# Gate units issued inside the ticks of the convolution and head units of a hybrid state-space, mixture-of-experts and sparse-projection layer

## The reference

```
zxbcdt = hidden_states @ in_proj_w.T
gate = zxbcdt[..., :DIN]
xBC = zxbcdt[..., DIN:DIN + CONV_DIM]
conv = conv_general_dilated(xBC, conv_w, ...)             # causal, 4 taps, one channel each
xBC = silu(conv + conv_b)
x, B, C = split(xBC)                                       # x: 128 heads of 64; B, C: 128 states a group
Y_diag = einsum('bhcij,bcjhd->bcihd', (C B^T) * L, x * dt) # inside a chunk
Y_off = einsum(C, states, exp(A_cumsum))                   # from the chunks before
y = Y_diag + Y_off + D * x
y = y * silu(gate)
y = y * rsqrt(mean(y * y over the group) + EPS) * norm_w
out = y @ out_proj_w.T
```

## Time and profile before

| what | us |
|---|---|
| median of 3 runs | 2342.14 (2337.01 to 2342.54) |
| the profiled execution, time | 2340.48 |
| its span, first to last instruction | 2338.4 |
| PE busy | 2096.4 (90%) |
| DVE busy | 1585.1 (68%) |
| ACT busy | 1231.7 (53%) |
| POOL busy | 1152.2 (49%) |

### The profile page before, as it was taken

How to read it: one execution, slowest core, us unless ns; L and a number is a source line. 1 busy time by engine, 2 the same in 40 slices (tenths; PEclk the granted TensorE clock), 3 DMA queues, 4 the chain that set the end, 5 groups by cost and what they waited for, 6 DMA issues and landing times.

```text
span 2338.4 us, 39600 instructions
## 1 busy us (share of the span) xinstructions
PE 2096.4 (90%) x11776; PEld 1731.7 (74%) x11776; DVE 1585.1 (68%) x2766; ACT 1231.7 (53%) x2680; POOL 1152.2 (49%) x987
## 2 busy tenths in 40 slices
PE   3889998989999989999998899899989888989897
PEld 2678777877777777777787778777777767767775
DVE  5797489739973996498659956984698463167314
ACT  2676367627762775377437744864476323522341
POOL 0377247814781578157716661765277414330332
PEclk7999999999999999999999999999999999999999
DMA  2343034203421342044113412331243027941894
GB/s 69 123 127 90 19 100 131 73 29 104 128 63 37 111 130 64 24 118 134 48 49 109 128 37 70 104 113 37 71 115 101 19 100 279 404 140 44 283 392 150
DMA packets 143765, 261.22 MB, mean 112 GB/s; under 512 B 19521, under 2 KB 35905, under 8 KB 143553
## 3 DMA queue, kind: packets, MB, share of 16 engines
q1 hardware_dynamic: 134848, 231.35, 31.2%
q0 software_dynamic: 7520, 24.65, 3.3%
q10 hardware_dynamic: 1184, 2.62, 0.3%
HBM read 233.38 MB, written 25.17 MB: 111 GB/s over the span
## 4 chain that ended last, share of the span: by engine, by line
PE 40%; issue 25%; POOL 21%; DVE 11%; ACT 1%; another core or an unknown queue 1%; POOLq 0%; DMA 0%; DVEq 0%; SPq 0%; ACTq 0%
PE bank L1475 25%; PE bank L1758 5%; POOL gt L681 5%; POOL Y L692 5%; POOL cv L699 4%; POOL Y L675 3%; PE bank L1608 3%; POOL wl L659 2%; PE bank L1770 2%; PE bank L1622 1%; DVE mem L1226 1%; POOL mem L650 1%; DVE Y L1184 1%; PE bank L1745 1%; DVE mem L1152 1%
## 5 line engine op out<-in xcount | busy, mean ns | idle before, releaser
L1475 PE MATMUL bank<-xh,wh 128*128 128x512 f32 x1288 | 522.2, 405 | 17.2 <-POOL wl L659 10.3
L1475 PE MATMUL bank<-xh,wl 128*128 128x512 f32 x1288 | 504.1, 391 | 0.0
L1475 PE MATMUL bank<-xl,wh 128*128 128x512 f32 x1288 | 503.5, 391 | 0.0
L659 POOL TENSOR_TENSOR wl<-raw,wh 128x512 fp32r<-128x512 f32 x144 | 183.9, 1282 | 511.1 <-ACT wh L857 510.5
L1184 DVE SCALAR_TENSOR_TENSOR Y<-bank,cpar,Y 128x511 f32<-128x511 f32 (+2 forms) x384 | 287.0, 747 | 21.3 <-ACT Y L874 11.1
L1475 PE MATMUL bank<-wh,ah 128*128 128x512 f32 x576 | 241.7, 420 | 65.7 <-DVE wl L1139 24.3
L1475 PEld LDWEIGHTS bank<-xh,wh 128*128 128x128 f32 x1288 | 243.2, 189 | 65.8 <-issue 12.2
L1475 PEld LDWEIGHTS bank<-xh,wl 128*128 128x128 f32 x1288 | 242.6, 188 | 52.6
L1475 PEld LDWEIGHTS bank<-xl,wh 128*128 128x128 f32 x1288 | 243.5, 189 | 45.1 <-issue 0.5
L1249 DVE TENSOR_TENSOR al<-Y,ah 128x512 fp32r<-128x512 f32 x128 | 108.8, 856 | 201.0 <-ACT ah L937 201.0
L650 POOL TENSOR_TENSOR mem<-mem,hpt 128x384 f32<-128x384 f32 x128 | 106.7, 834 | 275.9 <-DVE mem L1152 259.3
(11 more groups left out here) (211 smaller groups left out, 4228.7 us busy)
## 6 DMA issues: line engine op xcount, KB each, us to landing
mem<-c_rows SPq DMA_DIRECT2D x176, 256.0 KB, 3.6
mem<-wffn_d SPq DMA_DIRECT2D x62, 512.0 KB
E<-c_rows SPq DMA_DIRECT2D x256, 96.0 KB, 2.8
raw<-wconv_d SPq DMA_DIRECT2D x80, 256.0 KB, 2.8
cv<-c_rows SPq DMA_DIRECT2D x80, 256.0 KB, 3.6
raw<-wgate_d SPq DMA_DIRECT2D x64, 256.0 KB, 2.7
raw<-wout_d SPq DMA_DIRECT2D x64, 256.0 KB, 2.6
slots_y<-quad SPq DMA_DIRECT2D x62, 256.0 KB
```

What stands on the lines that cost most here:

```text
L659: inc(pool.tensor_tensor(wl[:, W_SLOT[p], :], raw[:, R_SLOT[p], :], wh[:, W_SLOT[p], :], ALU.subtract), w_lo)
L1475: got = mm(out, l, r, start=first and n == 0, stop=last and n == 2)
```

## The change

The gate units move. In the kernel after, gate unit n is issued in tick n+12, the out-projection in ticks 28 to 35, and a group has 36 ticks; ticks 12 to 19 have a convolution unit **and** a gate unit. The list `BIG` orders the 44 big units as they now come (conv 12, gate 0, conv 13, gate 1, ...), and the three banks go round in that order. PE issues a tick's gate unit behind the state sums and transposes, and ahead of diag and off. With it come:

- the tanh of the convolution's silu is written into the unit's own PSUM bank, and DVE ends the silu of every unit (`conv_ok`; POOL's two instructions for 11 of them go); the bank is free only after that, where it was free after the taps;
- the products with the masked C B^T move from DVE to POOL, the sum of squares from POOL to DVE;
- diag has one bank and is issued chunk by chunk, its two heads in turn; the transposes have two banks; there are eight `L` buffers;
- the exp of the row that scales off is made once for all groups ahead of the loop and loaded from a second tensor in device memory, `e_rows`;
- the x pieces 4 to 7 go by sequence first, which lets half of the out-projection's rows be ready early, and the weight pieces are loaded and rounded in a new order.

Lines of the kernel after that answer to lines before: 1482 for 1475 (the big matmuls), 1562 for 1565 (state sums), 1590 for 1593 (transposes), 1620 for 1608 (diag), 1634 for 1622 (off); on DVE 1196 for 1184 (taps), 1205 for 1193 (end of silu), 1164 for 1152, 1179 and 1184 for 1167 and 1172 (states), 1242 for POOL's 699.

```diff
-        TR, DG, ST, OF = 3, (4, 5), 6, 7
+        TR, DG, ST, OF = (3, 5), 4, 6, 7
...
-        EARLY = 9
-        conv_early = counted("conv_early", EARLY)
-        conv_vt = counted("conv_vt", NCONV - EARLY)
-        conv_late = counted("conv_late", NCONV - EARLY)
...
-        LR, ER = 6, 3
+        LR, ER = 8, 3
...
+        ULIST = [(t, b) for t in range(XT // 2) for b in range(BATCH)] \
+            + [(t, b) for b in range(BATCH) for t in range(XT // 2, XT)]
+        CLIST = [(t, b) for t in range(2) for b in range(BATCH)] + [(t + 2, b) for t, b in ULIST]
+        GATE_AT, OUT_AT = 12, 28
+        TICKS = OUT_AT + TT
+        BIG = []
+        for k in range(TICKS):
+            BIG += [("conv", k)] if k < NCONV else []
+            BIG += [("gate", k - GATE_AT)] if 0 <= k - GATE_AT < NGATE else []
+            BIG += [("out", k - OUT_AT)] if k >= OUT_AT else []
+        J = {what: j for j, what in enumerate(BIG)}
+
...
+        W_TICK = [0, 0, 1, 3, 5, 7, 7, 8, 9, 9, 10, 10, 11, 12, 13, 14, 15, 17, 20, 21, 22, 23, 24, 25, 26, 28]
...
-            if q < NCONV:
-                wait(eng, taps, i, 3 * q + 3)
-            elif q < NCONV + NGATE:
-                wait(eng, gate_ok, i, q - NCONV + 1)
-            else:
-                wait(eng, res_ok, i, q - NCONV - NGATE + 1)
+            kind, n = BIG[q]
+            wait(eng, dict(conv=conv_ok, gate=gate_ok, out=res_ok)[kind], i, n + 1)
...
+        def tr_bank(what):
+            return TR[TR_ORDER.index(what) % 2]
...
-            last = TR_ORDER[n - 1]
+            last = TR_ORDER[n - 2]
...
+                    u = k - A_ - 1
+                    if 0 <= u < UNITS:
+                        pair, b = unit(u)
+                        for h in range(2):
+                            n = 2 * u + h
+                            now(pool, decay_ok, i, n + 1)
+                            if n == 0:
+                                now(pool, g_ok, i, 2)
+                            inc(pool.tensor_tensor(L[n % LR], L[n % LR],
+                                    G[:, b * CH:(b + 1) * CH, :].rearrange("p c i -> p (c i)"),
+                                    ALU.mult), lg_ok)
...
-                    kc = k - 1
-                    if EARLY <= kc < NCONV:
-                        now(pool, conv_th, i, kc + 1)
-                        dst = piece(*conv_unit(kc))
-                        inc(pool.tensor_tensor(gt[:, kc % 2, :], dst, gt[:, kc % 2, :], ALU.mult), conv_vt)
-                        now(pool, conv_vt, i, kc - EARLY + 1)
-                        inc(pool.tensor_tensor(dst, dst, gt[:, kc % 2, :], ALU.add), conv_late)
-
...
-                    n = k - 3 - NCONV
-                    if BATCH <= n < NGATE:
-                        now(pool, sq_ok, i, n + 1)
-                        if n >= 2 * BATCH:
-                            now(pool, ss_add, i, n - 2 * BATCH + 1)
-                        inc(pool.tensor_tensor(acc[:, n % 2, :], acc[:, n % 2, :], sq[:, n % 2, :], ALU.add), ss_add)
...
+            n = step(nc.scalar.activation(v_hm, c_hm, ACT.Exp))
+            act.wait_ge(act_step, n)
+            act.dma_start(e_rows.rearrange("g h n -> (g h) n"), v_hm).then_inc(scr_rows, 16)
...
-                        e_arrived(act, i, u)
-                        inc(nc.scalar.activation(E[:, u % ER, :], E[:, u % ER, :], ACT.Exp), e_ok)
...
-                        inc(nc.scalar.activation(gt[:, kc % 2, :], src, ACT.Tanh, scale=0.5), conv_th)
+                        inc(nc.scalar.activation(bank[big_bank(J["conv", kc])][:, :], src, ACT.Tanh, scale=0.5), conv_th)
...
-                    if 0 <= kc < EARLY:
+                    if 0 <= kc < NCONV:
                         tile, b = conv_unit(kc)
                         dst = piece(tile, b)
                         now(dve, conv_th, i, kc + 1)
-                        inc(STT(dst, gt[:, kc % 2, :], 1.0, dst, ALU.add, ALU.mult), conv_early)
+                        inc(STT(dst, bank[big_bank(J["conv", kc])][:, :], 1.0, dst, ALU.add, ALU.mult), conv_ok)
 
...
-                        inc(STT(dst, dst, dcol[:, pair:pair + 1], bank[DG[u % 2]][:, :], ALU.mult, ALU.add), ydiag_ok)
+                        inc(STT(dst, dst, dcol[:, pair:pair + 1], bank[DG][:, :], ALU.mult, ALU.add), ydiag_ok)
...
-                        now(dve, e_ok, i, u + 1)
+                        e_arrived(dve, i, u)
...
-                    u = k - A_ - 1
-                    if 0 <= u < UNITS:
-                        pair, b = unit(u)
-                        for h in range(2):
-                            n = 2 * u + h
-                            now(dve, decay_ok, i, n + 1)
-                            if n == 0:
-                                now(dve, g_ok, i, 2)
-                            inc(TTn(L[n % LR], L[n % LR],
-                                    G[:, b * CH:(b + 1) * CH, :].rearrange("p c i -> p (c i)"),
-                                    ALU.mult), lg_ok)
...
-                    if NCONV <= k < NCONV + NGATE:
-                        n = k - NCONV
+                    n = k - GATE_AT
+                    if 0 <= n < NGATE:
                         now(dve, gate_th, i, n + 1)
-                        last = STT(gt[:, n % 2, :], gt[:, n % 2, :], 1.0, bank[big_bank(k)][:, :],
+                        last = STT(gt[:, n % 2, :], gt[:, n % 2, :], 1.0, bank[big_bank(J["gate", n])][:, :],
                                    ALU.add, ALU.mult)
                         inc(last, gate_ok)
+                    n = k - 3 - GATE_AT
+                    if BATCH <= n < NGATE:
+                        b = GATES[n][1]
+                        now(dve, sq_ok, i, n + 1)
+                        if n > BATCH:
+                            now(dve, ss_add, i, n - BATCH)
+                        inc(TTn(acc[:, b, :], acc[:, b, :], sq[:, n % 2, :], ALU.add), ss_add)
+                    for t, m in y_evac(k):
+                        now(dve, y_hi, i, 2 * t + m + 1)
+                        inc(TTn(al[:, m, :, :], rows_of(t, m), ah[:, m, :, :], ALU.subtract), y_lo)
...
-                    elif k < NCONV + NGATE:
-                        tile, b = gate_unit(k)
-                        half, col = tile // 4, tile % 4 * P
-                        if tile % 4 == 0 and b == 0:
-                            piece_split(pe, i, CONV + KT * half + KT - 1)
-                        big_bank_free(pe, i, k)
-                        for kt in range(KT):
-                            s = W_SLOT[CONV + KT * half + kt]
-                            last = three(out, xh[:, kt, b * SEQ:(b + 1) * SEQ], xl[:, kt, b * SEQ:(b + 1) * SEQ],
-                                         wh[:, s, col:col + P], wl[:, s, col:col + P], kt == 0, kt == KT - 1, False)
-                        inc(last, big_mm)
-                    else:
-                        t = k - NCONV - NGATE
...
+                    n = k - GATE_AT
+                    if 0 <= n < NGATE:
+                        tile, b = GATES[n]
+                        j = J["gate", n]
+                        half, col = tile // 4, tile % 4 * P
+                        if n % XT == 0:
+                            piece_split(pe, i, PNO["gate", KT * half + KT - 1])
+                        big_bank_free(pe, i, j)
+                        for kt in range(KT):
+                            s = W_SLOT[PNO["gate", KT * half + kt]]
+                            last = three(bank[big_bank(j)][:, :], xh[:, kt, b * SEQ:(b + 1) * SEQ],
+                                         xl[:, kt, b * SEQ:(b + 1) * SEQ],
+                                         wh[:, s, col:col + P], wl[:, s, col:col + P], kt == 0, kt == KT - 1, False)
+                        inc(last, big_mm)
 
                     u = k - D_
...
-                        if u >= 2:
-                            now(pe, ydiag_ok, i, u - 1)
+                        if u:
+                            now(pe, ydiag_ok, i, u)
                         else:
                             before(pe, ydiag_ok, i, UNITS)
-                        for h in range(2):
-                            for c in range(CH):
+                        for c in range(CH):
+                            for h in range(2):
                                 hs = slice(h * HD, (h + 1) * HD)
-                                last = mm(b4(DG[u % 2])[hs, c, :], xs[:, u % 3, c, hs],
+                                last = mm(b4(DG)[hs, c, :], xs[:, u % 3, c, hs],
                                           L[(2 * u + h) % LR][:, c * P:(c + 1) * P], start=True, stop=True)
```

More of the change, by code:

```diff
@@ L404, in conv_unit, with rows_gated @@
         def conv_unit(k):
-            return k // 2, k % 2
-        def gate_unit(k):
-            return unit(k - NCONV)
+            return CLIST[k]
+        GATES = ULIST
+        def rows_gated(eng, i, t, m):
+            now(eng, y_gated, i, max(n for n, (tile, b) in enumerate(GATES) if tile // 4 == m and b == t // CH) + 1)
         def piece(tile, b):
@@ L637, in _ @@
             with pool.Fori(0, GROUPS) as i:
```

(18 more changed lines are left out.)

174 lines of the change are left out of this document (84 added, 90 removed).

## The result

The kernel after takes 2516.35 us (median of 4 runs, 2505.77 to 2520.63) where the one before takes 2339.57: ratio 1.0751, 95% interval 1.071 to 1.0792. The forecast was 2472. The profiled execution took 2505.8 us, with a span of 2504.0.

What follows compares the result with a forecast made beforehand. PE, busy 90% of the span, was taken to bound the kernel. 207 + 112 + 12 + 10 + 16 - 164 - 62 = +131 us on 2340.5 gave 2472 us; the 8-in-10 range was 2350 to 2600.

Steps and rivals of the forecast that it cites:

- The wait: Ticks 13 to 19: PE's gate unit waits 3.7 us for DVE's end of silu, 7 times a group, +207 us.
- The clock: Ticks 13 to 19: matmuls behind each wait run at a slower clock, 2.0 us a tick, +112 us.
- Small ones: Minor effects across the group's ticks, entering the forecast sum as +12, +10 and +16 us, others taken as 0.
- (a): Ticks 0 to 5: convolution banks come free one tick later, 1.5 us a group, +12 us.
- (c): Ticks 9 to 12: ACT's two weight roundings a tick make conv 13 and gate 0 2 us late, +16 us.
- (b): Merged ticks: a 128x512 matmul behind a small one takes 0.31 instead of 0.23 us, 15 gates more, +10 us.
- What goes: PE's old waits at transposes and out-projection, 132.0 us, and the slow clock behind them, 32 us, vanish: -164 us.
- Diag in turns: Alternating heads overlaps the array halves in diag, gaining 0.56 us a unit, partly counted in ticks 20 to 26: -62 us.
- Ticks 20 to 27 about as long as before: Claim that these ticks, with products moved from DVE to POOL, keep about their old length.
- the first (the ring does not close): Rival: gates run inside the ticks, PE the only limit, 2153 us, or 2254 with half the wait; chance 0.14.
- the ring: Ticks 13 to 19: gate awaits end of silu, behind states needing this tick's state sums; next convolution queues behind the gate.
- The hold of DVE's sum of squares by POOL: Possible shared-port lockout ahead of DVE's states: a further 1.3 us hold would add 0.5 a tick, 28 us.

Runs made afterwards that it cites:

- e5: Kernel after with the x transposes issued nine times in ticks 13 to 19, useless work filling PE's wait for the end of silu: 2406.2 us.
- e3: Kernel after with ACT's tanh ahead of the convolution start and DVE's end of silu ahead of states and taps, behind tick 12: 2183.4 us.
- e4: Kernel after with gates back at ticks 20 to 35 and out-projection at 36 to 43, the rest of the change kept: 2153.0 us.
- e11: e4 with ACT's rounding of the gated rows moved ahead of the tick's square: 2151.5 us.
- e2: Kernel after with diag issued one head after the other again: 2544.8 us.
- e6: Kernel after with PE's gate unit behind diag and off in its tick instead of ahead of them: 2331.6 us.
- e9: e4 with diag issued one head after the other: 2214.1 us.

## Why the prediction was right

The named mechanism is what the runs show, and nearly all of the loss; its terms can be laid beside the rows:

- **The wait: +207, measured 212.** 3.79 us, 7 a group: 56 of the 80 waits for 1205.
- **The clock: +112, measured about 106 in the rows, 110 to 115 by e5.** In the second group the seven gate units take 5.42, 4.54, 4.54, 4.45, 5.42, 4.54, 4.54 us, 4.78 on the mean instead of the 2.95 of e5, and the seven diags 0.5 us more in all: 13.3 us a group. That it falls so near is partly luck: the old stalls gave 1.7 us (8.4 slow matmuls) on the mean and 2.8 at most, and the 2.0 a tick was chosen between them.
- **Small ones (a) and (c): +12 and +16, measured 24** (13.4 us of waits for `quad` in the first ticks of a group, and the other 24 waits for 1205, 10.4 us). (b), +10, was not measured apart; PE's busy time in e3, with merged ticks, is 10.0 us above that in e4, without them, which agrees with it.
- **What goes: -164, of which some 25 stayed.** The step failed where it says that the low half of the rows would come in time because it is ahead of the norm: 1245 still holds PE for 16.4 us and the last weight piece for 4.0. On ACT the rows stand behind a square that waits for DVE's sum of squares; I had looked at DVE's order alone, and e11 shows that ACT's order is a part of it. The slow clock behind these stalls, 32 us of the term, did not go everywhere either: in the out-projection's stretch of groups 3, 5 and 7 the granted clock is 0.97 over 58.7 us each, some 5 us in all. The rest of the 32 was not measured apart.
- **Diag in turns: -62, in PE's work -58 (e2) to -64** (128 x 0.5), but net of what it lets PE wait for only 28 to 36. The forecast took POOL for the next limit in ticks 20 to 26 and let 0.4 us a unit come through; DVE was the limit, as the next line shows. Diag takes 1.03 us, not under 1.0.
- **"Ticks 20 to 27 about as long as before" failed by a little**: the state sums wait 18.4 us in 32 times for DVE's states of the tick before. DVE is busy 41.49 of 43.20 us in that stretch, where the tick has gate, sum of squares and weight piece together. In the second group these ticks take 44.1 us, 47.4 before; without diag's 2.8 and the old waits' 2.2 they should have taken 42.4.

With what was measured the sum is 212 + 106 + 24 + 10 + 18 - 139 - 64 = +167, on 2340.5 that is 2507.5, against 2505.8 measured; the 10 and 27 us of the 139 are still the forecast's. The forecast's +131 was short by the 25 that stayed and the 18 that came, more than by anything else. The runs of the kernel lie between 2505.8 and 2520.6; the profiled one is the lowest of them, the median 10 us above it. So groups are 249.1 us apart and not 244, and of the 132 us of waits that were to be gone 20 are left. Two slips in the working change nothing: 366.39 is the start of the row behind the taps, which end at 366.47, and diag's term comes to 62.7.

Of the rivals, the first (the ring does not close) is what e3 shows: 2183.4, where I had worked out 2153 for PE as the only limit. The 30 us between them are about the same waits for 1245, the weight piece and the states (16.5, 4.0 and 17.0 us) that the forecast lacks. That e4, another kernel, takes 2153.0 is chance. The hold of DVE's sum of squares by POOL did not reach the ring: DVE stood 1.67 us ahead of the state sums.

The Trainium skill, "TensorE: Matmul & The Clock Gate", section "A second HAM failure mode: psum-queue depth-cycling", says that short idles between groups of matmuls make the clock go to and fro between its two levels: the trace agrees, with 0.85 in ticks 13 to 19 against 1.00 around them. e6 shows that not each such idle does it: behind five of the second group's seven waits of 1.90 to 1.97 us no matmul is slow.

What stays open is the distance of 30 us between e3 and e4, in part. By the reciprocals a group takes (1698.4 - 240.0) / 7 = 208.3 us in e3 and (1669.7 - 236.8) / 7 = 204.7 in e4, so the 3.6 us lie in the repeated part. PE's lists of waits account for half: e3 has 17.0 us of state sums that wait for DVE's states, which e4 has not, and 9.6 of gate units that wait for the end of silu where e4 has 1.4; e4 has 7.3 and 2.7 us in two entries of its own. The net is 15 us. PE's busy time is 10.0 us longer in e3, which fits the prediction's (b), the switches between small and large matmuls, but was not tested apart. The last 4 us no entry names.

## What to carry to other kernels

When two streams of work share a ring of buffers, write down for each use which earlier use it takes the buffer from, and where in the consumer's program of the same tick the releasing row stands. If it stands behind a row that needs this tick's product of the producer, the engines run in turns, however much room the sums of busy time show. Such a ring is broken by moving the releasing row (333 us here) or by a further buffer (224 us here, because the buffer was taken from the transposes and closed another ring there). Moving the row needs no buffer. Relieve an engine first and then look whether the merge is still needed: here it was not.

## What the runs showed of the hardware

**Two halves of the array.** Eight float32 matmuls of 64 columns (sixteen passes in the rows), heads in turn, take 1.03 us (after); head by head 1.52. Switching in and out included, that is 0.13 us a matmul against 0.19. The Trainium skill, "TensorEngine Tiling (Array Packing)", section "Key Properties", says that different tiles can load and multiply in parallel; the rows agree. Which head comes next decides, not the number of matmuls: e9, where PE is the limit, pays 61 us for the other order.

**DVE held by POOL.** In e4 POOL's gating product

```profile
424.39 1.68 POOL L714 TENSOR_TENSOR Y<-Y,gt 128x512 f32<-128x512 f32 x1 [1.89 <-DVE gt L1233]
```

runs beside DVE's rows. DVE's row 1245 with two SBUF inputs, 0.69 us where it runs alone (at 435.86), lasts until 0.54 us after POOL's end (424.39 + 1.68 = 426.07, 424.83 + 1.78 = 426.61):

```profile
424.23 0.68 DVE L1242 TENSOR_TENSOR cv<-cv,quad 128x512 f32<-128x512 f32 x1
424.83 1.78 DVE L1245 TENSOR_TENSOR al<-Y,ah 128x512 fp32r<-128x512 f32 x1
```

The Trainium skill, "SBUF — State Buffer", section "SBUF: two separate sides", says that a VectorE instruction with two SBUF inputs and a GpSimd instruction that reads SBUF shut each other out for a whole instruction; these rows agree. The rows with a PSUM operand (1205, 1233) keep their 0.68 us on the mean of all of them. In the merged kernel the tanh in PSUM makes the end of silu such a row: 0.68 us on the mean of all 160, where the old form with two SBUF inputs took 0.74 to 0.78.
